# Attention with values stationary and weights moving, and the weights normalised before their transposes

## The reference, cut to what matters

```python
H, D, window_size = (16, 64, 32)
xn = rms_norm(x)
qkv = xn @ w_qkv.T
q, k = apply_rope(q, cos, sin), apply_rope(k, cos, sin)
attn = jnp.einsum('bhqd,bhkd->bhqk', q, k) * scale
mask = (q_pos >= k_pos) & (q_pos - k_pos <= window_size)
attn = jnp.where(mask[None, None], attn, NEG)
attn = jax.nn.softmax(attn.astype(jnp.float32), axis=-1)
out = jnp.einsum('bhqk,bhkd->bhqd', attn, v)
return out.transpose(0, 2, 1, 3).reshape(B, T, H * D) @ w_out.T
```

## Time and profile before

| What | Value |
|---|---|
| Median of 3 runs | 504.74 us |
| Profiled execution, its own time | 509.57 us |
| Span of the profiled execution | 507.8 us |
| PE busy | 399.8 us (79%), 6608 matmul instructions |
| DVE busy | 321.9 us (63%) |
| ACT busy | 255.8 us (50%) |
| POOL busy | 179.1 us (35%) |
| Chain that ended last, by engine | PE 62%, DVE 15%, issue 6%, ACT 5%, POOL 4%, DMA 4% |
| Costliest group | POOL rope sum L1516, 64 × 1275 ns |

### The profile page before, as it was taken

One profiled execution on the slowest core, in us unless ns is written; L12 is line 12 of the kernel. 1 busy time (PEld: TensorE's weight loads), 2 busy tenths in 40 slices (PEclk: granted clock), 3 DMA queues, 4 the chain that ended last, 5 costly groups with the idle time before them and its releaser, 6 DMA issues.

```text
span 507.8 us, 16578 instructions
## 1 busy us (share of the span) xinstructions
PE 399.8 (79%) x6608; PEld 351.6 (69%) x6608; DVE 321.9 (63%) x1552; ACT 255.8 (50%) x642; POOL 179.1 (35%) x194
## 2 busy tenths in 40 slices
PE   2778799999999999968998402999995668999940
PEld 1667698898998989956785302998983445787840
DVE  2688777777777777867258692222129961688845
ACT  3356545655665656655538300454401464678547
POOL 2733444545444444433535480000006780000004
PEclk9999999999999999999999855899997975999865
DMA  8378855556556465530200403000000000000002
GB/s 258 84 182 226 256 139 134 131 124 145 119 128 145 108 150 134 120 82 3 84 1 0 94 1 93 2 1 1 0 3 0 1 0 1 1 2 2 1 2 83
DMA packets 28861, 38.58 MB, mean 76 GB/s; under 512 B 8368, under 2 KB 20784, under 8 KB 28656
## 3 DMA queue, kind: packets, MB, share of 16 engines
q1 hardware_dynamic: 28496, 36.47, 29.4%
q10 hardware_dynamic: 288, 1.05, 0.5%
HBM read 8.93 MB, written 3.28 MB: 24 GB/s over the span
## 4 chain that ended last, share of the span: by engine, by line
PE 62%; DVE 15%; issue 6%; ACT 5%; POOL 4%; DMA 4%; SPq 3%; POOLq 0%; ACTq 0%; DVEq 0%
PE QK L545 9%; PE VY L618 5%; PE O L596 4%; PE S L572 4%; PE PT L582 3%; PE O L687 3%; PE QK L877 3%; PE PT L605 2%; DVE keys_T L1094 2%; PE QK L751 2%; PE O L759 2%; DMA t_swap<-t_sin 2%; SPq L460 2%; PE QK L857 2%; DVE unread_tests L1204 2%
## 5 line engine op out<-in xcount | busy, mean ns | idle before, releaser
L1516 POOL TENSOR_TENSOR qk<-t_cos,t_swap 128x512 f32<-128x512 f32 x64 | 80.3, 1275 | 110.3 <-DMA t_swap<-t_sin 100.1
L1293 ACT ACTIVATE probs<-probs,negative_max 128x64 f32<-128x64 f32 x256 | 68.0, 338 | 40.2 <-DVE negative_max L948 40.2
L939 DVE TENSOR_TENSOR t_cos<-QK,cos 128x512 f32<-128x512 f32 x64 | 43.9, 687 | 28.4 <-POOL qk L1516 16.2
L948 DVE CUSTOM_DVE_ANT_0 probs<-S,masks 128x64 f32<-128x64 f32 x256 | 39.5, 220 | 8.3 <-PE S L572 8.3
L939 DVE TENSOR_TENSOR t_sin<-QK,sin 128x512 f32<-128x512 f32 x64 | 43.6, 681 | 0.0
L1553 POOL TENSOR_TENSOR rstd<-var_eps,minus_half 128x4 f32<-128x4 f32 x24 | 25.3, 1055 | 37.6 <-DVE var_eps L992 32.8
L1314 ACT COPY oT<-PT 128x512 f32<-128x512 f32 x32 | 18.7, 584 | 38.3 <-PE PT L605 38.3
L545 PE MATMUL QK<-xnT,wq 128*128 128x128 f32 x256 | 36.1, 286 | 1.3 <-ACT xnT L1324 0.7
L618 PE MATMUL VY<-wo,oT 128*128 128x128 f32 x256 | 34.8, 279 | 1.3 <-ACT oT L1314 0.7
L596 PE MATMUL O<-v_before,probsT 64*32 64x65 f32 x1024 | 29.0, 225 | 8.7 <-issue 7.0
L545 PE MATMUL QK<-xnT,wk 128*128 128x128 f32 x256 | 35.1, 282 | 0.6 <-DVE t_sin L939 0.6
(11 more groups left out here) (272 smaller groups left out, 1098.8 us busy)
## 6 DMA issues: line engine op xcount, KB each, us to landing
t_swap<-t_sin SPq DMA_DIRECT2D x128, 128.0 KB
v_before<-v_own SPq DMA_DIRECT2D x32, 132.0 KB
v_before<-v_own SPq DMA_DIRECT2D x62, 66.0 KB
late_tile<-late_weights SPq DMA_DIRECT2D x1, 1513.0 KB, 7.6
x_sb<-x SPq DMA_DIRECT2D x4, 256.0 KB, 5.9
inverse_dram<-invT SPq DMA_DIRECT2D x1, 1024.0 KB, 5.1
gram_dram<-gram SPq DMA_DIRECT2D x4, 256.0 KB, 2.3
invT<-inverse_dram SPq DMA_DIRECT2D x4, 256.0 KB, 5.5
```

The source lines that it names most:

```text
L939: last = nc.vector.tensor_tensor(dst[:, u % G, PAIRS * j:PAIRS * j + PAIRS], QK[j][:].rearrange("p (m t) -> p m t", m=PAIRS), table[:, tok ...
L948: last = nc.vector.tensor_tensor_reduce(out=probs[:, u % G, m, e, :], in0=S[:, e, m, :], in1=masks[:, min(u // G, 1), :], scale=-1.0, scal ...
L1293: last = nc.scalar.activation(probs[:, u % G, m, e, :], probs[:, u % G, m, e, :], ACT.Exp, scale=-1.0, bias=negative_max[:, u % G, e, m:m ...
L1516: nc.gpsimd.tensor_tensor(qk[:, h, c, WINDOW:WINDOW + P], t_cos[:, h, c], t_swap[:, h, c], ALU.add).then_inc(rope_done, 1)
```

## The change

The operands of the attention product change places: the values (64 keys × 64 channels of a head) are stationary and the weights (64 keys × 32 queries) move. The output then has the channels on the partitions and the queries along the columns, which is the form that the output projection wants, so `transpose_out` goes, and `keep_oT` copies out of the banks of `attend`. Since queries are no longer on the partitions there, the weights are divided by their sums earlier, in `probs`, between the exponentials and `transpose_probs`. The sums come from the exponentials themselves (`accum_out`), no longer from the column of ones, which is still written. On DVE `normalise` stands behind the rope products, for unit `u` in place of `u − 2`.

```diff
-        o_sb = sb("o_sb", [P, G, PAIRS, 2, D])
+        total = sb("total", [P, G, 2, PAIRS])
...
-        O_ps = O_banks[:, :, 0:PAIRS * DV].rearrange("p b (n d) -> p b n d", n=PAIRS)
+        O_ps = O_banks[:, :, 0:PAIRS * D].rearrange("p r (m q) -> p r m q", m=PAIRS)
...
             def transpose_probs(u):
-                pe.wait_ge(exp_done, 2 * u + 2)
-                wait(pe, oT_done, u - 1)
+                pe.wait_ge(probs_normalised, u + 1)
+                wait(pe, probsT_done, u)
...
-                wait(pe, o_kept, u)
+                wait(pe, oT_done, u)
...
-                            last = nc.tensor.matmul(O_ps[WINDOW * i:WINDOW * i + WINDOW, e, m, 0:D + 1],
-                                                    probsT[r, half(u), m, WINDOW * i:WINDOW * i + WINDOW],
-                                                    v[:, PAIRS * half(u) + m, 0:D + 1], start=True, stop=True)
+                            last = nc.tensor.matmul(O_ps[D * e:D * e + D, i // 2, m, WINDOW * (i % 2):WINDOW * (i % 2) + WINDOW],
+                                                    v[:, PAIRS * half(u) + m, 0:D],
+                                                    probsT[r, half(u), m, WINDOW * i:WINDOW * i + WINDOW], start=True, stop=True)
...
-                if 2 <= u < UNITS + 2:
-                    transpose_out(u - 2)
...
             def normalise(u):
-                dve.wait_ge(o_ps, u + 1)
-                wait(dve, oT_ps, u - 1)
-                totals = inv_total[:, u % G].unsqueeze(3)
-                nc.vector.reciprocal(totals, O_ps[:, :, :, D:D + 1]).then_inc(inverse_totals_done, 1)
+                dve.wait_ge(exp_done, 2 * u + 2)
+                nc.vector.reciprocal(inv_total[:, u % G], total[:, u % G]).then_inc(inverse_totals_done, 1)
                 dve.wait_ge(inverse_totals_done, u + 1)
-                nc.vector.tensor_tensor(o_sb[:, u % G].rearrange("p m e d -> p e m d"), O_ps[:, :, :, 0:D],
-                                        totals.broadcast_to([P, 2, PAIRS, D]), ALU.mult).then_inc(o_kept, 1)
+                by_bank = probs[:, u % G].rearrange("p m e k -> p e m k")
+                nc.vector.tensor_tensor(by_bank, by_bank, inv_total[:, u % G].unsqueeze(3).broadcast_to([P, 2, PAIRS, KEYS]),
+                                        ALU.mult).then_inc(probs_normalised, 1)
...
                     mask_scores(u)
-                if 2 <= u < UNITS + 2:
-                    normalise(u - 2)
                 if u >= 3:
                     residual(u - 3)
...
                     rope_products(u + 3)
+                if u < UNITS:
+                    normalise(u)
...
-                                                bias=negative_max[:, u % G, e, m:m + 1])
+                                                bias=negative_max[:, u % G, e, m:m + 1],
+                                                accum_out=total[:, u % G, e, m:m + 1])
...
             def keep_oT(u):
-                act.wait_ge(oT_ps, u + 1)
+                act.wait_ge(o_ps, u + 1)
...
-                nc.scalar.copy(oT[:, PAIRS * (u % G):PAIRS * (u % G) + PAIRS, :],
-                               PT[:].rearrange("p (n q) -> p n q", n=PAIRS)).then_inc(oT_done, 1)
+                to = oT[:, PAIRS * (u % G):PAIRS * (u % G) + PAIRS, :]
+                nc.scalar.copy(to.rearrange("p m (r q) -> p m r q", r=2), O_ps[:]).then_inc(oT_done, 1)
```

More of the change, by code:

```diff
@@ L334, in build @@
         o_ps = sem("o_ps")
-        o_kept = sem("o_kept")
-        oT_ps = sem("oT_ps")
+        probs_normalised = sem("probs_normalised")
         oT_done = sem("oT_done")
@@ L595, in attend @@
                             v = v_own[r, b % V_SLOTS, e] if i % 2 else v_before[r, b % 2, e]
-                            last = nc.tensor.matmul(O_ps[WINDOW * i:WINDOW * i + WINDOW, e, m, 0:D + 1],
-                                                    probsT[r, half(u), m, WINDOW * i:WINDOW * i + WINDOW],
-                                                    v[:, PAIRS * half(u) + m, 0:D + 1], start=True, stop=True)
+                            last = nc.tensor.matmul(O_ps[D * e:D * e + D, i // 2, m, WINDOW * (i % 2):WINDOW * (i % 2) + WINDOW],
+                                                    v[:, PAIRS * half(u) + m, 0:D],
+                                                    probsT[r, half(u), m, WINDOW * i:WINDOW * i + WINDOW], start=True, stop=True)
                 last.then_inc(o_ps, 1)
-            def transpose_out(u):
-                pe.wait_ge(o_kept, u + 1)
-                pe.wait_ge(probsT_done, min(u + 2, UNITS))
-                for m in range(PAIRS):
-                    last = nc.tensor.transpose(PT[:, m * P:(m + 1) * P],
-                                               o_sb[:, half(u), m].rearrange("p e d -> p (e d)"), ident[:])
-                last.then_inc(oT_ps, 1)
             def project_out(u):
@@ L623, in transpose_x @@
                 if q > 0:
-                    wait(pe, oT_done, q - 1)
                     pe.wait_ge(probsT_done, q)
@@ L1311, in keep_oT @@
             def keep_oT(u):
-                act.wait_ge(oT_ps, u + 1)
+                act.wait_ge(o_ps, u + 1)
                 wait(act, y_ps, u - 1)
-                nc.scalar.copy(oT[:, PAIRS * (u % G):PAIRS * (u % G) + PAIRS, :],
-                               PT[:].rearrange("p (n q) -> p n q", n=PAIRS)).then_inc(oT_done, 1)
+                to = oT[:, PAIRS * (u % G):PAIRS * (u % G) + PAIRS, :]
+                nc.scalar.copy(to.rearrange("p m (r q) -> p r m q", r=2), O_ps[:]).then_inc(oT_done, 1)
             def stage_x(q):
```

## The result

The changed kernel takes 518.59 us (median of 4 runs, 513.76 to 522.32) where the kernel before, run beside it, takes 504.73. The ratio is **1.022**, with a 95% interval of 1.014 to 1.030. A second set of runs of both kernels gave 1.020 (1.016 to 1.024). The forecast was 513.2 us, from +8.5 us; these 4 runs give +11 by their ratio, the second set +10.3. So the sign, the range and, as will be seen, the mechanism in the middle of the loop held. The forecast for the end of the loop did not, and the time that PE was to save per pass is not there.

The account below looks back on a forecast made before the run. PE bounds the kernel at 6.23 us per pass; after the change DVE's loop with its toll gives 6.48. Over 30 passes +7.5, exchange +1.5, loop end −0.5: +8.5 us on 504.74, so 513.2 us, range 502 to 522.

Parts of the forecast that it names:

- The toll on DVE: Product on the weights, two SBUF inputs, meets POOL's rope sum: 0.43 us per pass, ends 0 and 1.27.
- DVE's loop: Projection, rope products, normalisation, transposes, output projection: 5.92 us per pass without toll, 6.35 with it, longer than PE's own.
- PE's own 5.82: PE's work per pass: 5.96 less 0.36 of output transposes plus 0.22 for the attention product at 1.1 us.
- rival 1: Attention loop faster: toll 0, attention product stays 0.88, 6.0 us per pass, 499 us; chance 0.1.
- Passes at 6.48: Attention loop: 6.35 us with toll plus 0.13 of remaining issue stalls, against 6.23; +7.5 us over 30 passes.
- the 1.5 us for the exchange of halves: DVE's waits for POOL, held up by DMA, now delay normalisation and PE: 1.5 us added over the loop.
- The end of the loop: Behind the last attention product 1.6 us less, before the last transposes 0.93 and 0.7 more: net 0, to −1.
- Sums of the exponentials: ACT: 0.72 us more per pass, covered by residual and rope products, priced at nothing; without cover 0.36.
- rival 3: Attention product slow on PE: loads don't hide, 1.6 us, with stalls and toll +15.5, 520 us; chance 0.17.
- two quarters at once: Attention product: only two array quarters work together, product about 2.3 us, some 540 us; 0.03 of the 0.17.
- Rival 2: Attention loop unchanged: toll 0.15 to 0.25, product about 1.0, 6.2 us per pass, 505 us; chance 0.2.
- Rival 4: Exchange of halves rules alone: DVE's 11.7 us of waits reach PE whole, 521 us with toll; chance 0.03.

Follow-up runs that it names:

- the version in PSUM: Changed kernel with the inverse sums written to a free PSUM bank in place of SBUF; 510.83 us, ratio 1.010 to the kernel before.
- the product alone: Kernel before with only the attention product's operands exchanged (values stationary, weights moving), output without meaning; 514.8 us, ratio 1.012.
- the last units later: Changed kernel with inverse sums in PSUM and the last three units normalised behind the next masking on DVE; 509.04 us, ratio 1.005 to the kernel before.
- four quarters: Inverse sums in PSUM, both loop ends reordered, attention windows ordered 0, 2, 1, 3 to go round all array quarters; 506.17 us, ratio 0.998.
- both ends in order: Changed kernel, inverse sums in PSUM, x normalised first, last three units normalised later with the oT copy earlier; 507.6 us (1.001), again 506.97 us (1.001).
- x first: Changed kernel with inverse sums in PSUM and, in the first passes, normalise_x ahead of normalise on DVE; 508.9 us, ratio 1.003 to the kernel before.
- two quarters at a time: Inverse sums in PSUM, both loop ends reordered, all pairs of heads of one window one after the other; 517.44 us, ratio 1.025.

## Why the prediction was right, and where it was not

**The toll on DVE: right, in place and size.** The forecast charged 0.43 us per pass. Measured, as the mean of L946 less the 0.687 of the version in PSUM: 0.45 in the first execution, 0.31 in the second. Its upper end, one whole POOL row, is nearly reached at 1.71 − 0.69 = 1.02. By the Trainium skill (SBUF — State Buffer, section Who interferes with whom) a product with one SBUF input would not compete; the trace agrees, 687 ns on average and 0.69 us inside a running rope sum.

**DVE's loop: right.** 5.92 was the forecast without toll. Its pieces measure 5.16 + 0.69 = 5.85. With the toll it sets every pass in which the two meet, and PE waits for it before the transposes of weights, as foreseen.

**PE's own 5.82: the number right, with luck, and the saving not there.** The product was forecast at 1.1 and takes 1.09. Two terms that the sum left out nearly cancel: the later start, +0.13, and the values, which now start 0.81 us behind the second half of the projection (122.05 − 121.24), where transposes came 0.90 behind it, −0.08. But what 5.82 was compared with, 5.96, held a stall: without one the old product takes 0.78 and not 0.88, and the old pass 5.85. So the product costs +0.31, not +0.22, and −0.36 + 0.31 + 0.13 − 0.08 = 0.00: the undisturbed pass is 5.85 us before, and 5.86 in the version in PSUM. **The change saves PE nothing.** That is why taking away the toll brought no gain, and why rival 1, which asked for 6.0 per pass with no toll, was not to be had: in PSUM passes are 5.86 undisturbed and still 6.17 to 6.25 on average, as before. (DVE's loop, 5.85 without the toll, is as long as PE's own pass there. That PE's pieces alone fill it is shown by the product alone, whose transposes wait for no product on the weights: there too they start 1.09 behind the first instruction.)

The 0.13 is what the prediction had beside its sum, from TensorEngine Tiling (Array Packing) of the Trainium skill, section Key Properties: a switch of tiling mode drains the array. The Trainium skill gives no size for it, and the "some tenths" of the prediction were a guess, more than the 0.13. The rows fit the rule (scores on 64\*32, product on 64\*64, 0.79 for 0.66 in every pass with that switch), but the first load has also grown from 32 to 64 columns, and no run parted the two.

**Passes at 6.48: right, in part by luck.** 6.52 and 6.45. The loop with its toll was forecast at 6.35 and comes to 5.85 + 0.45 = 6.30 and 5.85 + 0.31 = 6.16; the disturbances that stay were forecast at 0.13 and are 0.22 and 0.29. From unit 9 to 27 the loss was 3.8 to 5.2 us, for 4.5 by 0.25 per pass, so the 1.5 us for the exchange of halves were not needed there. Up to unit 9 it was 3.1 and 2.1 us, for 2.2, but there the granted clock differed too: 0.89 and 0.94 from 20 to 50 us, where the kernel before had 1.00.

**The end of the loop, "net 0, to −1": wrong.** This is the step that failed. From unit 27 to the last projection the changed kernel takes 2.8 to 5.1 us more than the one before; by the forecast it would be 4 × 0.25 − 0.5 = +0.5. The prediction added up the pieces behind the last scores and did not ask what is queued behind the new wait. `normalise(u)` on DVE now waits for the exponentials of `u`, and the masking of `u + 1`, which the next exponentials need, stands behind it. In the middle that wait is covered by rope products of 2.4 us. In the last three units there are none. The chain of the changed kernel from 215 us (the x8 on ACT are four exponentials and the readings of their sums):

```profile
229.67 0.21 DVE probs L936
...
232.26 1.34 ACT probs L1280 x8
...
233.86 0.69 DVE probs L946
234.56 0.79 DVE bn_parts L970 x4
...
235.91 0.23 DVE probs L936
...
242.49 1.71 PE VY L609 x8
```

From one masking (229.67) to the next (235.91) are 6.24 us with the exponentials of one unit in one line with the normalisation and the first statistics of the norm. Moving the normalisation alone found the next holder (the copy on ACT) and brought 36.3 us from unit 27 to the last projection, for 37.7 in the second execution of the changed kernel; the same edit together with the PSUM operand cut that stretch from 38.8 to 34.9, as long as before.

And the thin stretch can cost a second time. Windows of 5 us of the changed kernel (busy us of each engine, then the granted clock, DMA share, GB/s):

```profile
230.00:235.00 5.00, 2.39 (x122) 2.09 (x123) 2.44 (x20) 3.71 (x18) 0.85 (x1) 1.00 0.21 53
235.00:240.00 5.00, 3.51 (x38) 3.15 (x31) 2.48 (x25) 3.39 (x18) 1.01 (x1) 0.66 0.00 0
240.00:245.00 5.00, 4.54 (x109) 4.30 (x110) 2.88 (x15) 1.39 (x3) 1.01 (x1) 0.68 0.02 3
```

PE, fed by exponentials, works 2.39 of 5 us, and then the granted clock drops to 0.66 and 0.68, a mix of 2.4 and 1.2 GHz; the kernel before stays at 1.00 from 215 to 235 us. An output projection takes 1.71 us in the chain in that stretch (242.49), and 0.89 at the full clock (216.55 in the same chain). The version in PSUM alone shows the same, worse (0.50 from 230 to 235 us), and with the last units later it is gone:

```profile
225.00:230.00 5.00, 2.16 (x53) 1.90 (x49) 3.22 (x20) 3.64 (x18) 0.44 (x2) 1.00 0.02 3
230.00:235.00 5.00, 4.37 (x128) 3.93 (x120) 1.96 (x8) 2.37 (x5) 0.63 (x1) 1.00 0.02 5
```

Not reliably: the execution with four quarters, with its ends in order, fell to 0.73 and 0.66 from 220 to 230 us. And the second execution of the changed kernel, with the same code, kept its full clock to the end of the loop. Its thinnest window:

```profile
235.00:240.00 5.00, 2.84 (x88) 2.67 (x91) 2.75 (x14) 2.73 (x11) 1.01 (x1) 1.00 0.01 3
```

(The version with the last units later kept it too, with 2.16 us of work in its thinnest window.) That parts clock and waiting. The 2.8 us of this second execution hold no loss of clock, so they are waiting; the 5.1 of the first are 2.3 more, which is what the clock can have cost in it. The stretch from unit 27 is 37.9 us with four quarters, where the clock fell, and 34.9 to 35.4 in the two executions with both ends in order, where it did not, so 2.5 to 3.0 there. In PSUM alone (38.8) and with x first (38.2, clock down to 0.58) it fell as well, so of the 3.9 us that the last units' edit took off the stretch, much may be clock and not order. These are single executions.

**Sums of the exponentials, "priced at nothing": probably wrong, and small.** The run without them points to some 2 to 4 us, with intervals that just meet.

**The rivals.** The slow product of rival 3 (1.6 us) is not what the change has, with its 1.09. Only the order with 16 matmuls in a row on two quarters has 1.79, and that version measures 1.025, without any toll (rival 3, with the toll, said 520 us). Its case of "two quarters at once" is disproved for the order used: going round all four changes nothing. Rival 2, no change, needed a toll of 0.15 to 0.25; it is what remains only at a toll of zero and with both ends of the loop reordered. Rival 4 needed DVE's waits for the rope sums to reach PE whole; they fell from 11.7 to 2.2 and 2.9 us.

So the loss of 10 to 11 us is about half toll, which the PSUM operand removes (5.0 us), and the rest the two ends of the loop, which their reordering removes (ratio 1.010 to 1.001); how it is shared between start, end and clock is not shown. What is then left is a kernel as fast as before, and none of the eleven runs beats it by more than its interval.

## What to carry to other kernels

Removing an instruction from the engine that bounds the loop is worth its time only after the instructions that take its place are priced on the same engine against a row without a stall: here 0.36 us of transposes (0.44 with the earlier start behind them) bought 0.44 us of slower product. Where a product on DVE has to read SBUF on both sides beside a busy POOL, a few values placed in a free PSUM bank take it out of POOL's way. And a wait moved earlier in an engine's program has to be followed in the passes that lack its cover, the first ones and the last ones, with everything queued behind it.

## What the runs showed of the hardware

- Tiled matmul instructions on four quarters of 64\*64 go at 14.6 ns each with 64 stationary and 32 moving columns (0.117 us for 8) when two or four matmuls in a row go to the same two quarters; with 16 in a row, at 25.6. Numbers between were not run. The old form on eighths of 64\*32, 65 moving columns, took about 0.63 us for its 64 when undisturbed, 10 ns each. The Trainium skill (TensorEngine Tiling (Array Packing), section Instruction Overhead) gives each matmul some 60 cycles of overhead, by an estimate from that figure 25 ns at 2.4 GHz. As a distance between instructions of the whole array the trace does not agree, with 14.6 and 10 ns; only the run with 16 in a row comes to it.
- Loads of the stationary operand are recorded with 105, 139 (133 in the second execution) and 198 ns for 32, 64 and 128 columns.
- Where a product on DVE with two inputs in SBUF meets a sum on POOL, both pay: the product 0.69 to 1.71 us, two rope sums 2.50 to 2.96, the small POOL row 0.46 to 0.91. With one input in PSUM neither does: 687 ns for the product, and 1278 ns for a sum where the kernel before has 1275.
- A slower PE takes up its disturbances. Mean pass less undisturbed pass: 6.23 − 5.85 = 0.38 us before, 6.46 − 6.30 = 0.16 with the slow product alone, and 6.56 − 6.54 = 0.02 with two quarters at a time, with the same exchange by DMA in all three.
- The granted clock at the end of the loop differs between executions of the same kernel: 1.00 throughout in one, 0.66 and 0.68 in two windows of 5 us in the other.
